# A graph network's first layer: ScalarE seeds PSUM with the second bias, GpSimd makes every second one-hot matrix

## What is computed

```
ei = concat([x[src], edge_attr], axis=-1)          # 50000 x (256 + 64)
core = maximum(ei @ W1 + b1, 0) @ W2 + b2
gate = sigmoid(ei @ Wg + bg)
msg = gate * core
agg = segment_sum(msg, dst)
out = layernorm(agg + x)
```

## Time and profile before

| what | value |
|---|---|
| timed runs | 1911.41, 1910.93 and 1906.35 us; median 1910.93 |
| span of the profiled execution, first to last instruction | 1691.9 us |
| time of the profiled execution itself | not recorded apart from its span |
| mean granted TensorE clock | 0.973 |
| busy: TensorE, VectorE, ScalarE, GpSimd | 1511.9, 1469.6, 1202.7, 1036.2 us |
| first layer's edge stage, by VectorE's gate sums | 109.7 to 803.4 us |

### The profile page before, as it was taken

How to read it: one execution, slowest core, us unless ns; L and a number is a source line. 1 busy time by engine, 2 the same in 40 slices (tenths; PEclk the granted TensorE clock), 3 DMA queues, 4 the chain that set the end, 5 groups by cost and what they waited for, 6 DMA issues and landing times. The chain is left out here.

```text
span 1691.9 us, 40433 instructions
## 1 busy us (share of the span) xinstructions
PE 1511.9 (89%) x10735; PEld 1378.6 (81%) x10735; DVE 1469.6 (87%) x3257; ACT 1202.7 (71%) x2896; POOL 1036.2 (61%) x1093
## 2 busy tenths in 40 slices
PE   6879999999999999999669688999998999999874
PEld 3669999999999999999459567787787887777653
DVE  4559999999999999999577689999999999999866
ACT  1458888888888888888056367777776767777573
POOL 0446666666666666664176577777777777777316
PEclk9989999999999999999979899999999999999888
DMA  4356666666666666665125787777777777777813
GB/s 135 138 184 186 187 186 186 186 187 186 187 187 188 185 188 185 187 184 145 33 82 191 221 245 220 231 228 231 227 228 224 225 229 227 229 226 223 281 46 97
DMA packets 164893, 318.92 MB, mean 188 GB/s; under 512 B 30231, under 2 KB 103928, under 8 KB 164436
## 3 DMA queue, kind: packets, MB, share of 16 engines
q0 software_dynamic: 66560, 219.06, 44.8%
q1 hardware_dynamic: 98132, 97.49, 18.7%
HBM read 291.90 MB, written 24.53 MB: 187 GB/s over the span
## 5 line engine op out<-in xcount | busy, mean ns | idle before, releaser
L493 POOL DMA_INDIRECT gath<-edge_in_tab,idx x392 | 413.6, 1055 | 270.5 <-DVE gate_in L933 207.6
L1226 PE MATMUL bank<-weighted,hot 128*128 128x260 f32 x880 | 238.6, 395 | 30.7 <-ACT hot L749 29.6
L506 POOL DMA_INDIRECT kept_more<-kv_tab,idx x176 | 195.5, 1111 | 60.6 <-issue 39.3
L1226 PE MATMUL bank<-w_lo,relu_hi 128*128 128x256 f32 x784 | 221.8, 283 | 0.0
L1226 PE MATMUL bank<-w_hi,relu_lo 128*128 128x256 f32 x784 | 221.7, 283 | 0.0
L1226 PE MATMUL bank<-w_hi,relu_hi 128*128 128x256 f32 x784 | 221.1, 282 | 0.0
L1226 PEld LDWEIGHTS bank<-weighted,hot 128*128 128x128 f32 x880 | 153.2, 192 | 53.4 <-ACT hot L749 36.7
L644 ACT ACTIVATE relu_hi<-bank 128x512 fp32r<-128x512 f32 x196 | 117.4, 599 | 81.4 <-PE bank L1226 81.4
L506 POOL DMA_INDIRECT hs<-kv_tab,idx x132 | 148.1, 1122 | 41.3 <-issue 36.3
L506 POOL DMA_INDIRECT xs<-kv_tab,idx x132 | 141.0, 1068 | 48.7 <-issue 22.7
L1229 PE MATMUL bank<-ident,gath 128*128 128x128 f32 x784 | 150.1, 273 | 10.6 <-DMA gath<-edge_in_tab,idx 10.6
(11 more groups left out here) (284 smaller groups left out, 4924.4 us busy)
## 6 DMA issues: line engine op xcount, KB each, us to landing
block_row<-row_tab SPq DMA_DIRECT2D x440, 64.0 KB
ea_in<-in_ea SPq DMA_DIRECT2D x392, 64.0 KB, 2.4
edge_in_tab<-node_row SPq DMA_DIRECT2D x26, 256.0 KB, 2.0
kv_tab<-qkv_row SPq DMA_DIRECT2D x25, 258.0 KB, 2.5
gath<-edge_in_tab,idx POOLq DMA_INDIRECT x392
xs<-in_x SPq DMA_DIRECT2D x1, 3328.0 KB, 15.2
v_in<-kv_tab SPq DMA_DIRECT2D x25, 130.0 KB, 2.1
rows_tab<-hs SPq DMA_DIRECT2D x25, 128.0 KB, 2.4
```

The costliest lines, as they stand in the source:

```text
L493: g.indirect_dma_start(gath[:, q, i, :], None, edge_in_tab, bass.IndirectOffsetOnAxis(ap=idx[:, half, q, i:i + 1], axis=0)).then_inc(gath_ ...
L506: g.indirect_dma_start(kept(u, 0, KVW)[:, i, :], None, kv_tab, bass.IndirectOffsetOnAxis(ap=idx1[:, half, u % BATCH, i:i + 1], axis=0)).th ...
L1226: return nc.tensor.matmul(out_, lhsT=lhs, rhs=rhs, start=start, stop=stop)
```

## The change

TensorE's two products of share and b2_parts go. In their place ScalarE copies the bias, held in all 128 partitions for both tiles (b2_rows), into the core's PSUM bank at the end of its step (`seed`), and the six products of each tile add onto what stands there. ScalarE makes one-hot matrices of even blocks alone, so dist has one buffer. GpSimd makes those of odd blocks with two comparisons, after the gathers of the chunk four later. GpSimd's loop is written out, and the gathers take their indices straight from src_chunk. Some semaphores of the prologue are merged to free numbers for the new ones.

```diff
-            b2_parts = sb(l0, "b2_parts", [2 * SHARES, HID], f32r)
+            b2_rows = sb(l0, "b2_rows", [P, 2, HID], f32)
...
-            def gather_node_rows(first, u, half, turn=0):
-                b, q = first + u, u % SLOTS
-                if q == 0:
...
-                    g.tensor_copy(idx[:, half, :, :], src_chunk[:, ds(b, SLOTS), :]).then_inc(idx_done, 1)
-                after(pool, gate_added, b - SLOTS + 1)
-                if q == 0:
-                    pool.wait_ge(idx_done, turn + 1)
-                pool.sem_inc(idx_seen, 1)
+            def gather_node_rows(c):
+                after(pool, gate_added, c - SLOTS + 1)
                 for i in range(2):
-                    g.indirect_dma_start(gath[:, q, i, :], None, edge_in_tab,
-                                         bass.IndirectOffsetOnAxis(ap=idx[:, half, q, i:i + 1], axis=0)).then_inc(gath_in[q], 16)
+                    g.indirect_dma_start(gath[:, c % SLOTS, i, :], None, edge_in_tab,
+                                         bass.IndirectOffsetOnAxis(ap=src_chunk[:, c, i:i + 1], axis=0)).then_inc(gath_in[c % SLOTS], 16)
+
+            def odd_one_hot(b):
+                if b % 2 == 1:
+                    after(pool, sum_ready, b - 1)
+                    for i in range(2):
+                        last = g.tensor_scalar(hot[:, 1, i, :], iota_node[:], rel_col[:, b, i:i + 1], None, ALU.is_equal)
+                    last.then_inc(pool_hot_done, 1)
...
-            for u in range(SLOTS):
-                gather_node_rows(0, u, 0)
-            with pool.Fori(0, (CHUNKS - SLOTS) // (2 * SLOTS)) as k:
-                for u in range(2 * SLOTS):
-                    gather_node_rows(2 * SLOTS * k + SLOTS, u, 1 - u // SLOTS, 2 * k + 1 + u // SLOTS)
+            chunks_and_blocks(pool, [(gather_node_rows, 0, CHUNKS), (odd_one_hot, 4, CHUNKS)])
...
-                after(act, hot_done, b - 1)
-                for i in range(2):
-                    last = s.activation(dist[:, b % 2, i, :], iota_node[:], ACT.Square, bias=rel_col[:, ds(b, 1), i], scale=-1.0)
-                last.then_inc(dist_done, 1)
+                if b % 2 == 0:
+                    after(act, hot_done, b // 2)
+                    for i in range(2):
+                        last = s.activation(dist[:, i, :], iota_node[:], ACT.Square, bias=rel_col[:, ds(b, 1), i], scale=-1.0)
+                    last.then_inc(dist_done, 1)
...
+            def seed(n):
+
+                if n < 2:
+                    act.wait_ge(row_ready, WPAD)
+                after(act, msg_done, n - 1)
+                s.copy(bank[4 + n % 2][:], b2_rows[:].rearrange("p i f -> p (i f)")).then_inc(seeded, 1)
 
             chunks_and_blocks(act, [(split_edges, 0, CHUNKS), (one_hot, 4, CHUNKS), (distances, 3, CHUNKS), (relu_inner, 2, CHUNKS),
-                                    (high_message, 4, CHUNKS), (gates, 3, CHUNKS)])
+                                    (high_message, 4, CHUNKS), (gates, 3, CHUNKS), (seed, 2, CHUNKS)])
...
+            def onto(out_, lhs, rhs):
+
+                return nc.tensor.matmul(out_, lhsT=lhs, rhs=rhs, start=False, stop=False, skip_group_check=True)
+
             def core(n):
+
+                pe.wait_ge(seeded, n + 1)
                 pe.wait_ge(relu_lo_done, n + 1)
                 for i in range(2):
                     to = bank[4 + n % 2][:, i * HID:(i + 1) * HID]
-                    mm(to, share[:], b2_parts[:], True, False)
                     for c in range(2):
                         tile = slice(c * CHUNK + i * P, c * CHUNK + (i + 1) * P)
-                        mm(to, relu_hi[:, n % 2, tile], w2_hi[:, c, :], False, False)
-                        mm(to, relu_hi[:, n % 2, tile], w2_lo[:, c, :], False, False)
-                        last = mm(to, relu_lo[:, n % 2, tile], w2_hi[:, c, :], False, c == 1)
+                        onto(to, relu_hi[:, n % 2, tile], w2_hi[:, c, :])
+                        onto(to, relu_hi[:, n % 2, tile], w2_lo[:, c, :])
+                        last = onto(to, relu_lo[:, n % 2, tile], w2_hi[:, c, :])
...
                 pe.wait_ge(msg_lo_done, b + 1)
-                pe.wait_ge(hot_done, b + 1)
+                if b % 2 == 0:
+                    pe.wait_ge(hot_done, b // 2 + 1)
+                else:
+                    pe.wait_ge(pool_hot_done, b // 2 + 1)
```

More of the change, by code:

```diff
@@ L117, in build @@
             msg_lo = sb(l0, "msg_lo", [P, 2, 2, HID], f32r)
-            dist = sb(l0, "dist", [P, 2, 2, P], f32)
+            dist = sb(l0, "dist", [P, 2, P], f32)
             hot = sb(l0, "hot", [P, 2, 2, P], f32r)
@@ L240, in build @@
         d_step = sem("d_step")
-        counted, cumulated, sel_ready, rows_ready, off_ready, cols_ready, meta_ready = (
-            sem(n) for n in ("counted", "cumulated", "sel_ready", "rows_ready", "off_ready", "cols_ready", "meta_ready"))
+        lists_made, tallies_made, meta_ready = sem("lists_made"), sem("tallies_made"), sem("meta_ready")
         w_hi_done, w_lo_done, wqkv_hi_done, wqkv_lo_done, bo_hi_done, bo_lo_done = (
@@ L249, in build @@
         gath_in, ea_arrived = sems("gath_in", SLOTS), sems("ea_arrived", SLOTS)
-        idx_done, ea_hi_done, ea_lo_done, z_ready, relu_hi_done, relu_lo_done, gate_done, core_ready = (
-            sem(n) for n in ("idx_done", "ea_hi_done", "ea_lo_done", "z_ready", "relu_hi_done", "relu_lo_done",
+        ea_hi_done, ea_lo_done, z_ready, relu_hi_done, relu_lo_done, gate_done, core_ready = (
+            sem(n) for n in ("ea_hi_done", "ea_lo_done", "z_ready", "relu_hi_done", "relu_lo_done",
                              "gate_done", "core_ready"))
@@ L607, in _ @@
             s.copy(w2_hi[:], w2_sb[:]).then_inc(w_hi_done, 1)
-            s.copy(b2_parts[:], b2_sb[:]).then_inc(w_hi_done, 1)
             def normed(done):
@@ L657, in distances @@
             def distances(b):
-                after(act, hot_done, b - 1)
-                for i in range(2):
-                    last = s.activation(dist[:, b % 2, i, :], iota_node[:], ACT.Square, bias=rel_col[:, ds(b, 1), i], scale=-1.0)
-                last.then_inc(dist_done, 1)
-            def one_hot(b):
-                act.wait_ge(dist_done, b + 1)
-                after(act, sum_ready, b - 1)
-                s.activation(hot[:, b % 2, :, :], dist[:, b % 2, :, :], ACT.Relu, bias=one_col[:], scale=-1.0).then_inc(hot_done, 1)
+                if b % 2 == 0:
+                    after(act, hot_done, b // 2)
+                    for i in range(2):
+                        last = s.activation(dist[:, i, :], iota_node[:], ACT.Square, bias=rel_col[:, ds(b, 1), i], scale=-1.0)
+                    last.then_inc(dist_done, 1)
+            def one_hot(b):
+                if b % 2 == 0:
+                    act.wait_ge(dist_done, b // 2 + 1)
+                    after(act, sum_ready, b - 1)
+                    s.activation(hot[:, 0, :, :], dist[:], ACT.Relu, bias=one_col[:], scale=-1.0).then_inc(hot_done, 1)
+            def seed(n):
[3 more added lines that the diff above has]
+                s.copy(bank[4 + n % 2][:], b2_rows[:].rearrange("p i f -> p (i f)")).then_inc(seeded, 1)
             chunks_and_blocks(act, [(split_edges, 0, CHUNKS), (one_hot, 4, CHUNKS), (distances, 3, CHUNKS), (relu_inner, 2, CHUNKS),
-                                    (high_message, 4, CHUNKS), (gates, 3, CHUNKS)])
+                                    (high_message, 4, CHUNKS), (gates, 3, CHUNKS), (seed, 2, CHUNKS)])
             act.wait_ge(lw_in, 3 * 16)
@@ L853, in _ @@
             step(v.tensor_scalar(neg_off[:], bank[2][0:1, 0:BLOCKS], -FAR, FAR, ALU.mult, ALU.add))
[L854 to L856 removed]
+            v.scalar_tensor_tensor(neg_off[:], in0=win_f[:], scalar=-float(P), in1=neg_off[:], op0=ALU.mult, op1=ALU.add).then_inc(lists_made, 1)
+            dve.wait_ge(w_hi_done, 3)
             v.tensor_tensor(w_node_lo[:], w_node[:], w_node_hi[:], ALU.subtract).then_inc(w_lo_done, 1)
             v.tensor_tensor(w_edge_lo[:], w_edge[:], w_edge_hi[:], ALU.subtract)
[L859 removed]
             v.tensor_tensor(w2_lo[:], w2_sb[:], w2_hi[:], ALU.subtract).then_inc(w_lo_done, 1)
@@ L1242, in _ @@
                 last = mm(bank[2][0:1, 0:BLOCKS], ones_c[0:HALF_C, 0:1], chosen[:, c, :], c == 0, c == 1)
-            last.then_inc(rows_ready, 1)
-            pe.wait_ge(off_ready, 1)
+            last.then_inc(tallies_made, 1)
+            pe.wait_ge(lists_made, 4)
             for i in range(2):
@@ L1269, in _ @@
                     last = mm(bank[3][0:HALF_B, cols], chosen[:, c, some], nat_f[:, 2, c, :], c == 0, c == 1)
-            last.then_inc(cols_ready, 1)
+            last.then_inc(tallies_made, 1)
             pe.wait_ge(meta_ready, 1)
-            pe.wait_ge(w_in, 9 * 16)
+            pe.wait_ge(w_in, 10 * 16)
             def transpose_rows(rows, source_done, freed, ready):
```

28 lines of the change are left out of this document (14 added, 14 removed).

## The result

The changed kernel takes 1951.74 us (median of 4 runs, 1940.46 to 1958.98) beside 1911.17 us for the kernel before on the same chips: a ratio of 1.0208, 95% interval [1.0172, 1.0244]. It is 40.6 us slower, where 27 us faster was forecast.

What follows compares the result with a forecast made beforehand. TensorE was taken to pace a 3.557 us step; afterwards the largest engine floor, taken as 3.42 us, would gain (3.557 - 3.42) x 195 = 27 us: span 1665, time 1884 us, range 1868 to 1928.

Steps and rivals of the forecast that it cites:

- The base: Whole kernel: profiled span 1691.9 us plus a fixed 219.0 us around it gives the timed 1910.93 us.
- steady state: Edge pipeline before the change: TensorE busy all the time and pacing a step of 3.557 us, VectorE 93.5% busy.
- The step that failed: GpSimd's: GpSimd's loop of gathers and comparisons: its own busy time was put at 3.33 to 3.51 us a step.
- four floors: Edge step: the largest of VectorE 3.36, TensorE 3.29, ScalarE 3.13 and GpSimd 3.33 to 3.51 us sets it.
- The seed: ScalarE's bias copy into PSUM: 0.53 us each, offset by removed one-hot work, so no net change and no added wait.
- The floor without the two products: Edge step once TensorE's two products go: TensorE needs 3.29 us, but VectorE's 3.36 us comes first.
- VectorE is held by GpSimd: Rival: comparisons delay VectorE's ea_parts and msg_lo, step 3.59 to 3.70 us, time 1917 to 1939 us; chance 0.20.
- The gap stays: Rival: VectorE's 0.22 us before hs is register load, not slack; step 3.53 us, time about 1911 us; chance 0.08.
- GpSimd the bound: Rival: comparisons cost 0.75 us each, so GpSimd sets a step of 3.61 us, time 1921 us; chance 0.07.
- dear seed: Rival: ScalarE's bias copy costs 1.06 us, so its step is 3.66 us, time 1931 us; chance 0.05.
- The granted clock: Sign in the edge stage: a clock under 1.00 would move TensorE's floor and make the whole forecast wrong.

Runs made afterwards that it cites:

- e0: The kernel before the change, run again unchanged: 1909.66 us, ratio 0.9997.
- after: The changed kernel, with the whole change made to the kernel before: 1951.74 us, ratio 1.0208.
- e14: The changed kernel with all one-hot matrices on ScalarE and no GpSimd comparisons; seed and written-out loop without the semaphore count stay: 1957.5 us, ratio 1.0311.
- e3: The kernel before with GpSimd's gather loop written out, without index copies or semaphore count; no seed, no comparisons: 1995.28 us, ratio 1.0412.
- e8: e3 with the semaphore count alone put back between the wait and the gathers: 1907.02 us, ratio 0.9993.
- e15: e12 plus GpSimd's comparisons for odd blocks, written into a spare tile that nobody reads: 1977.54 us, ratio 1.0386.
- e12: The changed kernel with all one-hot matrices on ScalarE, no GpSimd comparisons, and the semaphore count put back; seed and written-out loop stay: 1870.65 us, ratio 0.984.
- e1: Seed alone: the changed kernel with GpSimd's loop and ScalarE's one-hot matrices of the kernel before: 1877.47 us, ratio 0.9825.
- e16: The changed kernel with the semaphore count and one comparison in every step instead of two in every second: 1887.75 us, ratio 0.9902.

## Why the prediction was wrong

**The base.** "I put 1910.93 - 1691.9 = 219.0 us around the span and hold it fixed" was wrong. Some 1.8 us lie there in e0 and 1.9 in after. The trace showed a faster execution, with a step of 3.557 us where the timed kernel needs 3.712. The "steady state" of a TensorE that is always busy is not that of the timed runs: e0 has it at 96.6% in the window of the earlier trace rows and 88.0% for VectorE.

**The step that failed: GpSimd's.** The prediction priced GpSimd by its own time ("GpSimd, idle for a third of the step now, becomes a third engine at the floor") and took the largest of four floors as the step. Of what the diff removes from GpSimd's loop it named the index copy alone; the count, and with it the moment at which each gather starts, it put at nothing. GpSimd's own time was about right: a comparison takes 0.61 us for the 0.47 taken, inside the bounds 0.43 to 0.75, and gathers restart 0.17 us behind it, where 0.97 was taken. But no floor set the step; waits between the engines did. In place of 3.42 us the step is 3.911, and e14, with the count gone and no comparison, has 3.888. Two things in GpSimd's program are each enough: the lost count (e3 beside e8) and a pair of comparisons in every second step (e15 beside e12). Both move the gathers in the step; that this is how they cost is the reading that fits best, and is not shown by a run of its own.

**What held.** The seed: 0.58 us for 128x512, and ScalarE's next operation follows 0.51 us behind its start in e12 (401.68 to 402.19), where 0.53 was taken. The floor without the two products: the median step of e1 and e12 is 3.35 us, worked out from the gate sums' starts, where 3.36 was forecast for VectorE. The mean steps are 3.523 and 3.512, because some steps stay long. In the two traces the seed alone gains (3.712 - 3.523) x 195 = 36.9 us in the stage, of which the unchanged second layer, 7.0 us longer in e1's trace, hides a part (1875.4 less 796.5 against 1071.9).

**The rivals.** None was the cause. "VectorE is held by GpSimd" is not what happens in after: msg_lo meets a comparison in 1 step and ea_parts in 44 of 196, and their medians stay 0.69 and 0.42 us. One such step (VectorE's and GpSimd's timeline):

```profile
403.85 1.20 POOL L491 TENSOR_SCALAR hot<-iota_node,rel_col 128x128 fp32r<-128x128 f32 x2
...
404.99 0.42 DVE L923 TENSOR_TENSOR ea_parts<-ea_in,ea_parts 64x256 fp32r<-64x256 f32 x1
405.44 0.69 DVE L953 TENSOR_TENSOR msg_lo<-msg,msg_hi 128x512 fp32r<-128x512 f32 x1
```

In e15 a comparison often starts first and VectorE is held: msg_lo takes 0.82 us and ea_parts 0.56 there. Summed over the stage VectorE loses 11 us so, of the 98 us by which e15's stage is longer than e12's. In e16 VectorE often starts first, and the comparison is the one that stretches:

```profile
398.93 0.75 DVE L955 TENSOR_TENSOR msg_lo<-msg,msg_hi 128x512 fp32r<-128x512 f32 x1
399.29 0.87 POOL L492 TENSOR_SCALAR hot<-iota_node,rel_col 128x128 fp32r<-128x128 f32 x1
...
402.66 0.63 POOL L492 TENSOR_SCALAR hot<-iota_node,rel_col 128x128 fp32r<-128x128 f32 x1
```

GpSimd goes from 0.63 to 0.87 us, VectorE from 0.69 to 0.75. The Trainium skill, "SBUF — State Buffer", section "Who interferes with whom", has an exclusive lock: whichever issues first holds the shared ports for its whole instruction, and the other blocks. Here the later one is GpSimd, which by that rule would have stood 0.39 us, until msg_lo ends at 399.68; it took 0.24 longer and msg_lo 0.06, so the trace agrees in who pays and only in part in how much. "The gap stays" is refuted by the 3.35 us of e1, "GpSimd the bound" by its 67.06 us of work in the 100 us above, "dear seed" by 0.58 us. The granted clock, named as what would make all wrong, is 0.98 in after's window of the earlier trace rows and 0.98 in e0's, nearly always the higher of its two levels, so it does not tell them apart; e3 has 1.00 there and is slowest but one.

**What stays open.** That GpSimd's gathers hold TensorE's signals is read from many traces and from their place in the step, but no run changed the hold alone, and no run is fast without the count. Good places were 0.81, 0.89 and 1.88 us, bad ones 0.27, 1.23, 1.37 and those that swing; why just these is not explained. Also open is why the trace that the prediction read has no late signal at all, though 312 of its products end inside a second gather: from 120 to 680 us z's signal comes 0.01 us on average behind its product's modelled end there, 0.33 in e0, 0.72 in after (of the signals on record). So a gather under way is not enough for a late signal. The seed with both the count and the wait for ea_parts was not tried.

## What to carry to other kernels

Check that the span of the profile you read agrees with the timed runs before you take a step length from it; here a difference of 11% was a faster execution, not time around the span. When an edit rewrites the loop of an engine that issues transfers, ask when each transfer now starts, down to instructions that seem to do nothing, and do not price the engine's busy time alone. And take a change of several parts apart first: the seed here was worth 1.6 to 1.9%, and the new loop by itself cost more than twice that.

## What the runs showed of the hardware

- One GpSimd instruction that only counts on a semaphore, between a wait and an indirect gather, moved the gather from 0.27 to 0.81 us behind the release and the kernel from a ratio of 1.0412 to 0.9993 (e3 and e8).
- In e3 TensorE's signal of core came 1.8 us behind its product's modelled end (638.66 for 636.84), and four signals within 0.22 us. Over all runs but the trace that the prediction read, 87% of the signals on record whose product ends inside a chunk's second gather were over 0.2 us late, 16% of those inside the first.
- ScalarE copies 128x512 from SBUF into PSUM in 0.58 us, its gate of the same size from SBUF to SBUF takes 0.63; a GpSimd comparison of 128x128 takes 0.61 us.
